# An attention and expert kernel: GpSimd's gathers placed last in each head's turn, and three batches normalised one head from the end

## What is computed

```python
# attention: 16 heads per batch, each with two softmaxes over queries and keys of width 8
o = a1 - lam * a2                                      # a_i = softmax(q_i k_i^T) v
o = _rms_norm(o, sub_norm_w, EPS) * (1.0 - LAMBDA_INIT)
o = o.transpose(0, 2, 1, 3).reshape(B, N, C) @ w_proj.T + b_proj
# experts: the two best of 8 for each token, eo is the experts' output, one row per slot
out = (g1 * keep1)[:, None] * eo[f1] + (g2 * keep2)[:, None] * eo[f2]
x = x + attention(xn) + experts(xn)
```

## Time and profile before

| | us |
|---|---|
| median of 3 runs | 1813.76 |
| lowest and highest of them | 1813.74, 2590.47 |
| the profiled execution, time | 1814.34 |
| the profiled execution, span in the trace | 1812.5 |

### The profile page before, as it was taken

How to read it: one execution, slowest core, us unless ns; L and a number is a source line. 1 busy time by engine, 2 the same in 40 slices (tenths; PEclk the granted TensorE clock), 3 DMA queues, 4 the chain that set the end, 5 groups by cost and what they waited for, 6 DMA issues and landing times.

```text
span 1812.5 us, 39337 instructions
## 1 busy us (share of the span) xinstructions
PE 1719.5 (95%) x15555; PEld 748.2 (41%) x15555; DVE 1487.0 (82%) x1727; ACT 1403.3 (77%) x2639; POOL 578.5 (32%) x1065
## 2 busy tenths in 40 slices
PE   6869999999999999999999999999999999999898
PEld 5437888888885222222222222222222222222226
DVE  7767777777767999998999989899999999999913
ACT  4535455445435999999999989999999999999993
POOL 1474221222100345455454554542121211112230
PEclk9989999999999999999999999999999999999999
DMA  7564232212203111111111111110101011100002
GB/s 238 198 223 138 93 111 91 67 63 91 85 24 106 40 39 43 41 34 44 40 44 41 34 40 44 41 38 22 31 24 30 25 28 27 27 11 5 5 1 94
DMA packets 92281, 109.66 MB, mean 61 GB/s; under 512 B 17473, under 2 KB 67265, under 8 KB 92097
## 3 DMA queue, kind: packets, MB, share of 16 engines
q1 hardware_dynamic: 85952, 90.36, 15.9%
q0 software_dynamic: 6144, 16.79, 3.2%
HBM read 72.77 MB, written 33.82 MB: 59 GB/s over the span
## 4 chain that ended last, share of the span: by engine, by line
PE 78%; ACT 15%; POOL 3%; DVE 2%; issue 1%; DMA 1%; SPq 0%; ACTq 0%; DVEq 0%; POOLq 0%
PE banks L1222 25%; PE banks L1210 15%; ACT arena_t L779 13%; PE banks L1261 10%; PE banks L1241 10%; PE banks L1192 10%; POOL arena_v L557 2%; PE banks L1281 2%; ACT o_raw L758 2%; PE banks L1115 2%; PE banks L1343 2%; PE banks L1161 1%; PE banks L1126 0%; DMA arena_x<-x_in 0%; PE banks L1334 0%
## 5 line engine op out<-in xcount | busy, mean ns | idle before, releaser
L992 DVE TENSOR_REDUCE row_half<-banks 128x2 f32<-128x1024 f32 x1024 | 1189.3, 1217 | 153.7 <-PE banks L1192 149.8
L779 ACT ACTIVATE arena_t<-banks 128x512 f32<-128x512 f32 x2048 | 1085.4, 599 | 59.8 <-PE banks L1210 34.0
L1222 PE MATMUL banks<-arena_t,v_ring 128*17 128x256 f32 x8192 | 643.5, 386 | 37.3 <-ACT o_raw L758 37.2
L1222 PEld LDWEIGHTS banks<-arena_t,v_ring 128*17 128x17 f32 x8192 | 136.2, 95 | 416.7 <-issue 241.4
L1210 PE MATMUL banks<-arena_q 50*128 50x512 bf16 x960 | 286.3, 384 | 0.6 <-ACT arena_t L779 0.6
L1210 PE MATMUL banks<-qk_ring 50*128 50x512 bf16 x896 | 266.2, 386 | 5.2 <-DVE arena_r L1040 2.5
L1192 PE MATMUL banks<-arena_q 48*128 48x512 bf16 x960 | 269.6, 384 | 0.0
L1192 PE MATMUL banks<-qk_ring 48*128 48x512 bf16 x896 | 251.1, 384 | 2.9 <-DVE row_half L992 1.4
L743 ACT ACTIVATE arena_t<-banks 128x512 f32<-128x512 f32 x128 | 76.5, 598 | 206.0 <-PE banks L1241 197.3
L1261 PE MATMUL banks<-w_parts,hidden_parts 128*128 128x256 f32 x1536 | 196.3, 286 | 0.0
L1261 PEld LDWEIGHTS banks<-w_parts,hidden_parts 128*128 128x128 f32 x1536 | 187.1, 192 | 13.5 <-issue 13.4
(11 more groups left out here) (147 smaller groups left out, 1356.6 us busy)
## 6 DMA issues: line engine op xcount, KB each, us to landing
expert_rows<-arena_r SPq DMA_DIRECT2D x16, 512.0 KB, 3.0
q_stack<-arena_q SPq DMA_DIRECT2D x8, 768.0 KB, 4.7
k_stack<-arena_q SPq DMA_DIRECT2D x8, 768.0 KB, 3.4
v_heads<-arena_v SPq DMA_DIRECT2D x4, 1088.0 KB, 5.6
v_ring<-v_heads SPq DMA_DIRECT2D x64, 68.0 KB, 2.9
arena_x<-x_in SPq DMA_DIRECT2D x4, 1024.0 KB, 6.3
token_rows<-arena_x SPq DMA_DIRECT2D x4, 1024.0 KB, 7.8
arena_v<-w_gate_in SPq DMA_DIRECT2D x4, 1024.0 KB, 6.2
```

Of the source, the lines that this page charges most:

```text
L779: nc.scalar.activation(probs[:, kt % PSLOTS, q, :], banks[:, ST_BANKS[ring_place(i) % 3], :], ACT.Exp).then_inc(exp_done, 1)
L992: nc.vector.tensor_reduce(halves[:, :, j // 2], banks[:, SMAX_PAIRS[m % 2]:SMAX_PAIRS[m % 2] + 2, :], AX.X, ALU.max, negate=True).then_inc ...
L1222: mm = pe.matmul(banks[QUAD * q:QUAD * q + VP, OT_BANK, columns], v_ring[:, g % SLOTS, kt, :], probs[:, kt % PSLOTS, q, columns], start=(k ...
```

## The change

It does two separate things.

1. In GpSimd's turn for head g the order gather, add_bias, combine becomes combine, add_bias, gather. The work is the same; the gathers are issued last.
2. All four pieces of the first norm move later: `mean_square` to place 0 of DVE's step 62, the root on ACT to after exponential 7 of step 62, `norm_factors` to place 4 of DVE's step 62, and the three multiplications on GpSimd to after `square_sums(61)`.

```diff
+        NORM_FIRST_AT = G - 2
...
                 square_sums(g)
-                if g < NT:
-                    gather(g)
-                    add_bias(g)
                 if 1 <= g <= NT:
                     combine(g - 1)
-                if g == G - SLOTS - 1:
+                if g < NT:
+                    add_bias(g)
+                    gather(g)
+                if g == NORM_FIRST_AT - 1:
                     for b in range(B - 1):
                         pool.wait_ge(inv_ready_first, 1)
...
-                if g == G - SLOTS:
-                    root_mean_square(FIRST, 1)
+                    if g == NORM_FIRST_AT and kt == 1:
+                        root_mean_square(FIRST, 1)
...
-                    if g == G - SLOTS and j == 2 * TB - 1:
+                    if g == NORM_FIRST_AT and j == 0:
                         mean_square(FIRST, G - H)
-                    if g == G - SLOTS + 1 and j == 4:
+                    if g == NORM_FIRST_AT and j == 4:
                         norm_factors(FIRST, 1)
```

## The result

The changed kernel takes 1809.01 us, the median of 10 runs (1807.14 to 1811.01), against 1814.18 us of before, also of 10. The ratio is 0.9970, with a 95% interval of 0.9962 to 0.9979: 5.2 us less, clear of noise and far within 2%. The profiled execution took 1807.14 us, with a span of 1805.3 us.

What follows compares the result with a forecast made beforehand. PE and ACT, passing work back and forth, were taken to bound the kernel, with gathers delaying ACT once a head. 1814.34 - 2.1 - 2.8 = 1809.4, less 0.58 to the median: 1809 us; own range 1803 to 1816, wider 1796 to 1823.

Steps and rivals of the forecast that it cites:

- the two terms: GpSimd's new order, -2.1 us over 32 heads, and the later norm of three batches, -2.8 us.
- I take it as hidden: Old place: the second gather's packets fall where PE stands 0.74 us anyway for the `o_raw` copy, so cost nothing.
- Part 1: GpSimd's turn, gathers issued last: 0.55 us a head at the new place, -2.1 us; bounds -19.7 and +18.7 us.
- 0.615: Microseconds by which each of the first 32 heads, with gathers, was longer than the later ones before the change.
- 0.3 us of slack: Ahead of the `o_turned_sb` read, just behind the gathers' new place: absorbs 0.3 of 0.85 us delay a head.
- Rival A: New place is good: gathers cost 0 to 0.2 us a head there, total 1793 to 1798 us; chance 0.20.
- Rival B: New place exposes both gathers: with 1.1 us a head, +15.5 us and 1826 us; chance 0.20.
- Rival C: Packets aren't what costs, only that GpSimd makes gathers in a head, wherever: part 1 is 0, 1811 us; chance 0.10.
- Part 2, steps 60 and 61: Table loads and root leave step 60, DVE's reciprocal and a shorter instruction leave step 61: -2.9 us each.
- Part 2, step 62: The loads and root come here, where ACT has only exponentials and nothing hides them: +3.1 us.
- (a): Transpose of head 63's maxima, now behind the norm factors, still in time for step 63, with 3 us to spare.
- (b): GpSimd's three multiplications, 11.4 us, done by 1753.6, ahead of the next inversion at 1755.5: 1.9 us to spare.

Runs made afterwards that it cites:

- narrow rows: Changed kernel with gather rows of 64 bytes in place of 1 KB for heads 2 to 31, from other places of the table: 1811.8 us, ratio 0.9973.
- SP's load: Changed kernel with GpSimd's old order and the second gather of heads 2 to 31 replaced by a plain 128 KB load from SP's queue: 1797.5 us.
- order only: Kernel before with only GpSimd's new order (combine, bias, gather), norm left as it was: 1811.4 us, ratio 0.9979.
- the norm alone: Kernel before with only the later norm of three batches, GpSimd's turn left as it was: 1814.4 us, ratio 0.9994.
- split turn: Changed kernel with GpSimd's turn as bias, first scale, first gather, second scale, two additions, second gather: 1800.7 us, ratio 0.9921.
- spaced kernels: Changed kernel with both scales and the first addition between the two gathers, second addition and bias last: 1794.1 us; with 12 added matmuls in step 62, 1791.3 us.
- no gathers: Changed kernel with gathers for the first two heads only, combine adding what stands in its buffers: 1797.1 us, ratio 0.9902.
- the 12 matmuls: Changed kernel with 12 unread 512-column matmuls in PE's wait for the root in step 62: 1808.9 us, ratio 0.9968.
- the kernel with one gather: Changed kernel without the second gather of heads 2 to 31: 1795.5 us with the new order, 1797.1 us with GpSimd's old order.

## Why the prediction was right, and where it wasn't

**The time.** Forecast 1809, measured 1809.0; the kernel got faster by a third of a per cent, as said. But the two terms were wrong in opposite directions: -2.1 and -2.8 were forecast, -3.8 and -1.1 measured by the ratios of the two halves, -5.8 and -0.9 by the copies of the profiled executions. The agreement to the digit is luck.

**Where the loss is, and that the gathers make it: right.** After the change the 33 heads are 618.73 - 33 x 18.33 = 13.8 us above the pace without gathers; leaving the gathers of 30 heads out removed 12.2 of them. That a combine and SP's loads cost nothing held as well.

**"Now the first gather costs about 0.55 us", and of the second one's packets "I take it as hidden": wrong, and the main fault.** The first gather alone costs nothing at the old place. I had read the wait at exponential 4 as the work of the packets that begin just ahead of it. In that same microsecond GpSimd was issuing the second gather (1004.13 to 1005.08 in the earlier trace rows), and I didn't weigh that row. What costs is a second gather issued 1.4 us behind the first. The narrow rows rule out the bytes, and SP's load rules out a second transfer as such. In the head that was looked at PE was on time up to the first late exponential, so what is delayed is ACT's start on a score. What remains is either GpSimd's second issue while the first gather is under way, or two gathers following each other in its queue, of any size. The waits at the old place began ahead of the second gather's packets, which speaks for the issue; no run separated the two.

**Part 1, 0.55 us a head at the new place: the mechanism wrong, the size near.** The wait did move to exponentials 10 to 12, as the prediction said it would if the gathers were the cause. Measured 0.41 for the pair. With 0.41 in place of 0.55 the term would be (0.41 - 0.615) x 32 = -6.6 us; the copies show -5.8 in 33 heads, the runs of order only -3.8 (-2.0 to -5.4). Of the 0.3 us of slack ahead of the `o_turned_sb` read only 0.1 us a head was used up: ACT's idle time there fell from 10.6 to 7.6 us. The delay itself was then about 0.5 us, not 0.85. Of the 5.8 us, 1.8 are no property of the new place as such. Before, the two heads around 1065 us were slow. Three `o_raw` copies of before, timeline of ACT:

```profile
1044.09 0.58 ACT L758 COPY o_raw<-banks 128x512 f32<-128x512 f32 x1
1063.44 0.59 ACT L758 COPY o_raw<-banks 128x512 f32<-128x512 f32 x1
1083.73 0.58 ACT L758 COPY o_raw<-banks 128x512 f32<-128x512 f32 x1
```

A window of before between the last two:

```profile
1065.00:1068.00 3.00, 3.00 (x24) 0.44 (x20) 1.61 (x2) 1.93 (x5) 0.72 (x1) 0.50 0.18 41
```

They took 39.64 us, 1.8 more than two average heads of 18.94, and PE's granted clock was at 0.5. ACT's longest wait, 1.2 us, stands just ahead of it. The profile of the norm alone, which has the same order, shows the same two heads (39.65 us); the profiles with the new order have 37.05 and 37.19 us there. I left this fall in the average of 0.615 without seeing it. Whether the gathers bring it on no run shows; it is missing in every profile of a kernel with the new order.

**Rival A** (a good place exists) was nearer to the truth than I gave it: the gathers can cost nothing, but mainly by their distance. Their place has a small part at most: in the split turn, 3.75 us apart with the first 1.4 us ahead of the copy, 0.10 us a head stay, and in the spaced kernels nothing does. A gather alone at the places of the split turn was not run. (A's range was also added up 2 us short: a cost of nothing gives 1791, not 1793.) **Rival B** (both exposed) rested on the same wrong reading. **Rival C** named an "only the fact that GpSimd makes gathers in a head" cost; one gather in a head costs nothing.

**The Trainium skill,** SBUF — State Buffer, section "SBUF: two separate sides", by which a transfer's packets can't hold up PE or ACT, I had set against the trace. The runs side with it on that point: packets of a gather or of SP's load beside it cost nothing. The waits in the two stretches, which I took as evidence against it, come from something that section doesn't speak of. The Trainium skill, DMA: Bandwidth & Descriptors, section "SWDGE vs HWDGE vs iDMA", says that GpSimd's DMAs have their descriptors written by GpSimd itself into rings in SBUF, in one queue, and that SP's don't take that path. That fits the two runs of narrow rows and of SP's load; that writing them is what delays ACT's start on PE's scores, no run here shows.

**Part 2, steps 60 and 61: right.** Forecast 18.4 and 18.0 to 18.2, measured 18.41 and 17.87. My ground for step 61 was incomplete: of its 2.9 us only some was DVE's reciprocal. Before shows PE's clock at 0.5 behind PE's wait of 1.45 us for DVE, which ended at 1719.68, and that went too:

```profile
1720.30:1723.50 3.20, 3.20 (x21) 1.12 (x24) 1.72 (x3) 1.54 (x4) 3.20 (x2) 0.50 0.00 0
```

**Part 2, step 62: the term that was mis-sized.** "So nothing hides them: +3.1 us" and the copies 20.3 us apart; measured 22.56. The 2.2 us are PE's clock, which fell to 0.5 behind its wait of 2.92 us. How long it stays low varies: in no gathers and narrow rows it was at 0.5 for half as long, and step 62 took 21.54 us. The prediction named this as what would make it wrong and then priced it at nothing. With the 12 matmuls the step took 20.32 us: without the fall, the term was exact, and part 2 is -3.1 us (72.14 against 75.27) in place of -0.9. As it stands, the norm alone is worth 1.1 us with an interval that holds zero.

**The covers held.** (a) The transpose of head 63's maxima was at 1729.02, SP's last issues ended at 1734.5, and step 62 ended at 1741.8. (b) GpSimd's three multiplications ran from 1737.65 to 1749.07, the inversion came at 1751.12: 2.1 us to spare, forecast 1.9. Timeline of DVE:

```profile
1729.02 0.21 DVE L1008 STREAM_TRANSPOSE neg_blocks<-neg_parts 128x32 bf16<-128x32 bf16 x1 [0.24 <-DVE arena_r L1067]
...
1751.12 0.25 DVE L1055 RECIPROCAL inv_sum<-o_turned_sb 128x16 f32<-128x16 f32 x1 [17.12 <-ACT o_turned_sb L769]
```

Timeline of POOL:

```profile
1737.65 11.42 POOL L355 TENSOR_TENSOR arena_v<-arena_v,arena_r 128x2048 f32<-128x2048 f32 x3
```

From the first table load to the next exponential are 3.12 us (1723.78 to 1726.90), as before the change (1707.43 in the earlier trace rows to 1710.55): the two loads and the root, and next to nothing else.

## What to carry to other kernels

Before you blame an operation for a stall that begins beside it, list everything that was issued in the same microsecond, and take the suspects out one at a time: here the kernel with one gather overturned a reading that gave the right total. Where GpSimd makes its own transfers, put other work of its own between them; here three instructions in between took 19 us off the 33 heads of before, moving the pair as a whole 6, of which 2 were a fall of PE's clock. And price a standstill of PE at the standstill plus what its clock may do afterwards (0 to 2.4 us here), and, where PE is the one that others wait for, try to give it something to do.

## What the runs showed of the hardware

- Two indirect gathers of GpSimd, issued 1.4 us apart, lengthen a head by 0.56 (0.62 with a fall of the clock) or 0.41 us. One gather lengthens it by nothing that the copies show. Two 3.7 us apart add nothing in the spaced kernels and 0.10 us a head in the split turn.
- In the head that was looked at, PE starts the score on time, and ACT starts on it 0.95 us behind PE in place of 0.48.
- Smaller rows don't make the delay smaller: with 64 bytes in place of 1 KB the same pair cost (623.91 - 606.50) / 30 = 0.58 us. That it is more than with full rows (0.41) I can't explain.
- A plain load of 128 KB from SP's queue beside a gather costs nothing.
- After a wait of 2.92 us PE's granted clock was 0.5 for 6.8 us, and ACT lost 2.2 us by it. In two other profiles the clock was low for half as long behind the same wait, and 1.2 us were lost (21.54 against 20.32). Behind a wait of 2.51 us it stayed at 1.00 in before and fell in order only. With 12 matmuls of 2.75 us in that wait it stayed at 1.00, in both kernels that had them.
